# Two buffers of gathered sums in the pass over groups, and the gather issued ahead of the list writes

## What is computed

```
x1 = x + (sum over edges and self loops of alpha * xl[src]) @ W_up
s  = layernorm(x1) @ expert_tokens.T            # 8 scores, top 2
x2 = x1 + sum over the 2 experts of 0.5 * mlp_e(layernorm(x1))
```

## Time and profile before

| | us |
|---|---|
| median of three runs | 2071.64 |
| the profiled execution, its own time | 2070.93 |
| its span in the profile | 2069.0 |
| TensorE matmuls busy | 1657.0 (80%) |
| VectorE busy | 1310.2 (63%) |
| GpSimd busy | 783.9 (38%) |
| ScalarE busy | 774.3 (37%) |

### The profile page before, as it was taken

How to read it: one execution, slowest core, us unless ns; L and a number is a source line. 1 busy time by engine, 2 the same in 40 slices (tenths; PEclk the granted TensorE clock), 3 DMA queues, 4 the chain that set the end, 5 groups by cost and what they waited for, 6 DMA issues and landing times.

```text
span 2069.0 us, 27936 instructions
## 1 busy us (share of the span) xinstructions
PE 1657.0 (80%) x8625; PEld 1335.5 (65%) x8625; DVE 1310.2 (63%) x2446; ACT 774.3 (37%) x1342; POOL 783.9 (38%) x758
## 2 busy tenths in 40 slices
PE   4999999999586636887788783888888788788886
PEld 3788888888332325676567663667666676666665
DVE  4555555555266555666668773777777777776775
ACT  3444444443133520000100002555555555555554
POOL 1211222112488002554456542443444443443453
PEclk9999999999888776888788886999999999999999
DMA  9344444441544235899888854566665665566421
GB/s 242 85 135 124 119 119 119 119 133 47 158 119 113 74 126 129 223 227 217 200 219 216 206 157 119 157 193 177 180 175 166 170 177 171 168 171 179 115 52 34
DMA packets 128365, 311.76 MB, mean 151 GB/s; under 512 B 69455, under 2 KB 75981, under 8 KB 116651
## 3 DMA queue, kind: packets, MB, share of 16 engines
q1 hardware_dynamic: 58809, 181.56, 34.1%
q0 software_dynamic: 66208, 108.34, 19.0%
q10 hardware_dynamic: 3234, 20.48, 3.2%
HBM read 188.85 MB, written 138.85 MB: 158 GB/s over the span
## 4 chain that ended last, share of the span: by engine, by line
PE 47%; DMA 14%; DVE 13%; POOL 11%; issue 9%; ACT 5%; SPq 2%; DVEq 0%; POOLq 0%; ACTq 0%
PE psum L1531 12%; PE psum L1533 10%; PE psum L1532 10%; DMA agg<-node_table,from_idx 6%; DVE xt_lo L1448 4%; PE psum L1556 4%; DVE xb L1467 3%; DMA out<-xb,idx_in 3%; PE psum L1549 3%; POOL lists L651 2%; POOL agg L634 2%; PE psum L1812 2%; POOL xls L616 2%; DMA xb<-rows_x,idx_in 2%; POOL td L620 2%
## 5 line engine op out<-in xcount | busy, mean ns | idle before, releaser
L1531 PE MATMUL psum<-xt_hi,st_w 128*128 128x256 f32 x528 | 179.5, 340 | 142.5 <-DVE xt_lo L1448 138.7
L696 POOL DMA_INDIRECT out<-xb,idx_in x132 | 184.8, 1400 | 142.0 <-DVE xb L1467 109.5
L855 ACT ACTIVATE xt_hi<-psum 128x512 fp32r<-128x512 f32 x264 | 150.8, 596 | 228.8 <-PE psum L1812 215.7
L1448 DVE TENSOR_TENSOR xt_lo<-psum,xt_hi 128x512 fp32r<-128x512 f32 x264 | 175.6, 684 | 89.9 <-ACT xt_hi L855 77.6
L1531 PEld LDWEIGHTS psum<-xt_hi,st_w 128*128 128x128 f32 x528 | 103.7, 196 | 186.1 <-DVE xt_lo L1448 178.5
L827 ACT ACTIVATE aggt_hi<-psum 128x500 fp32r<-128x500 f32 x40 | 22.7, 587 | 450.0 <-PE psum L1728 450.0
L1288 DVE TENSOR_TENSOR cx<-cx,psum 125x512 f32<-125x512 f32 x160 | 108.8, 680 | 121.5 <-PE psum L1533 119.1
L959 DVE TENSOR_TENSOR axt_lo<-psum,axt_hi 128x500 fp32r<-128x500 f32 x160 | 108.5, 678 | 108.9 <-ACT axt_hi L728 95.0
L849 ACT ACTIVATE xn<-xb 128x1024 f32<-128x1024 f32 x132 | 156.3, 1232 | 54.8 <-DMA xb<-rows_x,idx_in 54.5
L1812 PE MATMUL psum<-ident,xn 128*128 128x128 f32 x1056 | 154.3, 281 | 23.1 <-ACT xn L849 23.1
L687 POOL DMA_INDIRECT xb<-rows_x,idx_in x132 | 140.1, 1062 | 85.6 <-POOL xb L683 54.0
(11 more groups left out here) (280 smaller groups left out, 4413.7 us busy)
## 6 DMA issues: line engine op xcount, KB each, us to landing
rows_x<-cx SPq DMA_DIRECT2D x20, 1806.0 KB
cx<-in_x SPq DMA_DIRECT2D x20, 1792.0 KB
ax<-in_x SPq DMA_DIRECT2D x19, 1792.0 KB
st_half<-experts SPq DMA_DIRECT2D x66, 512.0 KB
node_table<-trow ACTq DMA_DIRECT2D x19, 896.0 KB
node_table<-xld SPq DMA_DIRECT2D x10, 500.0 KB
st_half<-experts SPq DMA_DIRECT2D x66, 64.0 KB
rows_x<-cx SPq DMA_DIRECT2D x20, 209.6 KB
```

Of the source, the lines that this page charges most:

```text
L696: pool.indirect_dma_start(out=out[:, :], out_offset=bass.IndirectOffsetOnAxis(ap=idx_in[:, t % NI, s:s + 1], axis=0), in_=xb[:, b, s, 0:D] ...
L855: act.activation(xt_hi[:, 2 * q:2 * q + 2, :].rearrange("p k n -> p (k n)"), T_R[q % 2], ACT.Copy).then_inc(r_hi, 1)
L1448: dve.tensor_tensor(xt_lo[:, 2 * q:2 * q + 2, :].rearrange("p k n -> p (k n)"), T_R[q % 2], xt_hi[:, 2 * q:2 * q + 2, :].rearrange("p k n ...
L1531: pe.matmul(out_ap, left[0], right[0], start=start, stop=False, skip_group_check=True)
```

## The change

`agg` gets two buffers, chosen by g % 2, and a semaphore for each. A gather waits on `c_atp` for the transposes of the group two before instead of the one before. On GpSimd `gather_rows(g + 2)` stands ahead of `enlist(g - 1)`. `turns_p`, a semaphore that nothing waits on, is dropped, and its increments go to `turns`, on which nothing waits either.

```
-            ("agg", [P, J, HID], F32),
+            ("agg", [P, 2, J, HID], F32),
...
-        agg_loaded, list_put = sem("agg_loaded"), [sem("list_put0"), sem("list_put1")]
+        agg_loaded = [sem("agg_loaded0"), sem("agg_loaded1")]
+        list_put = [sem("list_put0"), sem("list_put1")]
...
-        turns, turns_p = sem("turns"), sem("turns_p")
+        turns = sem("turns")
...
             def gather_rows(g):
-                wait(pool, c_atp, KH * g)
+                wait(pool, c_atp, KH * (g - 1))
                 for j in range(J):
                     pool.indirect_dma_start(
-                        out=agg[:, j, :], out_offset=None, in_=t_half,
+                        out=agg[:, g % 2, j, :], out_offset=None, in_=t_half,
...
-                    ).then_inc(agg_loaded, 16)
+                    ).then_inc(agg_loaded[g % 2], 16)
...
             for g in range(NG):
                 if g >= 1:
                     rstd_c(g - 1)
-                    enlist(g - 1)
                 if g + 2 < NG:
                     gather_rows(g + 2)
+                if g >= 1:
+                    enlist(g - 1)
...
             def turn_agg(g):
-                pe.wait_ge(agg_loaded, 16 * J * (g + 1))
+                pe.wait_ge(agg_loaded[g % 2], 16 * J * (g // 2 + 1))
...
-                        last = pe.transpose(T_C[m][:, P * j:P * (j + 1)], agg[:, j, 128 * m:128 * (m + 1)],
+                        last = pe.transpose(T_C[m][:, P * j:P * (j + 1)], agg[:, g % 2, j, 128 * m:128 * (m + 1)],
```

More of the change, by code:

```diff
@@ L198, in build @@
             at3,
-            ("cx1", [P, J, ROW], F32), ("cx2", [P, J, ROW], F32), ("agg", [P, J, HID], F32),
+            ("cx1", [P, J, ROW], F32), ("cx2", [P, J, ROW], F32), ("agg", [P, 2, J, HID], F32),
             ("aggt_hi", [128, 2, KH, G], F32R), ("aggt_lo", [128, 2, KH, G], F32R))
@@ L583, in body @@
                 pool.wait_ge(map_put, 16 * (CPG * g + 1))
-                pool.sem_inc(turns_p, 1)
+                pool.sem_inc(turns, 1)
                 pool.tensor_copy(idx_now[:, 0:CPG], scat_idx[:, bass.ds(CPG * g, CPG)])
```

## The result

The changed kernel takes 2005.69 us (median of four runs, 2003.32 to 2012.03), beside 2072.32 us for the kernel before in the same runs. The ratio is 0.9681, 95% interval 0.9639 to 0.9723. The forecast was 2000 us.

A forecast was written before the change was run, and what follows sets the result against it. It took late gathered sums, issued behind list writes that wait for slot numbers, to bound pass C. From 2070.93 us, -6.2 for group 0 and -65.3 for 18 shorter periods gave 1999.4, say 2000 us; range 1977 to 2045.

The forecast's parts named there:

- What bounds the kernel before: Pass C: TensorE waits 76.4 us for gathered sums from group 1 on; the gather stands behind list writes awaiting slot numbers.
- Group 0: Start of pass C: the gather for group 1 goes out early, its 6.19 us wait goes; -6.2 us, bounds 0 and -7.6.
- The gather's place and landing: GpSimd issues it from 1.45 us after the score sum; sums land at 17.9 or 22.4, needed at 26.
- What is moved behind it: GpSimd's list writes lose nothing, the slot numbers coming at T + 7.6; VectorE's 11.1 us wait for the root goes.
- The new period: 18 periods of pass C fall from 22.53 to 18.9 us each, -65.3 us; bounds 17.56 and 22.53.
- (a): TensorE and VectorE limit in pass C: 18.5 us a period, the mean of five with little waiting, from 17.56 up.
- (b): DMA limit in pass C: share 0.83 over 422.54 us, read as 18.5 us of work for each of 19 groups.
- Its signs: Pass C: score sums some 340 us apart, `agg` waits under 10, slot wait under 3, DMA share near 0.97, 245 GB/s.
- Compute alone: Rival, pass C: DMA packs well and the period falls to 17.56 us, 1975 us in all; chance 0.15.
- The chain of store and load: Rival, SyncE: each load waits for a store to land, a hole of about 2.5 us, period 21.0, 2037 us; chance 0.23.
- No change: Rival, pass C: early gathers still wait for DMA engines behind loads of x, only group 0 gains, 2065 us; chance 0.06.
- Slower: Rival, pass C: gathers mixing with store and load lower the rate to 190 GB/s, 24.4 us a group, 2098 us; chance 0.06.

The follow-up runs named there:

- e2_order_only: Against the kernel before: gather ahead of the list writes, still one buffer of sums; 2015.34 us, ratio 0.9762.
- e1_buffers_only: Against the kernel before: two buffers of sums, gather still behind the list writes; 2058.5 us, ratio 0.9974.
- e6_late_gather_half_load: Two buffers, gather still behind the list writes, as in e1_buffers_only, with x loaded for two of four nodes from group 3 on; 2008.92 us, ratio 0.9713.
- e3_half_load: Changed kernel with x loaded for only two of four nodes of a partition from group 3 on; 1958.76 us, ratio 0.9503.
- e8_store_on_act: Changed kernel with the stores of a group's rows issued by ScalarE instead of SyncE; 1998.97 us, ratio 0.9652.
- e10_changed_again: The changed kernel run once more, unchanged, beside other kernels; 2002.79 us, ratio 0.9684.
- e4_split_halves: Changed kernel with each store and each load of x cut in halves, each half load behind its half store; 1995.39 us, ratio 0.9668.
- e7_more_bytes: Changed kernel with 0.92 MB of x copied from HBM to HBM beside each load of x, and waited for; 2044.00 us, ratio 0.9877.
- e5_by_node: Changed kernel with x loaded so that neighbouring partitions read neighbouring rows, same bytes and piece size; 2000.26 us, ratio 0.9670.
- e9_flat_load: Changed kernel with x from group 3 on loaded in one 16 KB piece for each partition instead of four of 4 KB; 2005.10 us, ratio 0.9681.
- e11_experts_late: Changed kernel with the weights of four of seven expert slots loaded behind the last load of x and split in the last two groups; 2013.61 us, ratio 0.9726.

## Why the prediction was right, and where it was off

*What bounds the kernel before.* Right. The sums were late because the gather was issued behind the list writes and their wait. e2_order_only shows it by the order alone, e1_buffers_only by the buffer alone. The loads of x in front of the late gather had a part in it (e6_late_gather_half_load).

*Group 0.* -6.2 us forecast, -7.4 measured (25.65 to 18.27), near the end of -7.6 that took in the slow matmuls behind the wait: the wait of 6.19 us is gone, and TensorE is busy 1.2 us less (19.46 to 18.27).

*The gather's place and landing.* Right. It was to be issued from T + 1.45 and is, from T + 1.7 (1047.39 for a score sum at 1045.71); the sums are there in time in all groups but one, which waits 2.9 us.

*What is moved behind it.* Right. The list writes start 3.12 us behind the gather, at the slot numbers; VectorE's wait for the root fell from 11.1 us to 0.8. e6_late_gather_half_load shows that this part can matter more than it seemed: with fewer bytes in the old order VectorE waits 37.2 us for the root, more than TensorE's 25.0 for the sums.

*The new period.* The term of the sum that was mis-sized: 18.9 us forecast, 19.34 measured (19.11 and 19.30 in two more profiles), 18 x 0.44 = 8 us too little, against which group 0 gave back 1.2. Both limits under it were off, and in opposite ways. (a) The compute limit was read as 18.5, and 17.56 as its lower bound, from the few periods of the old kernel without much waiting. With the DMAs relieved it is 16.93 (e3_half_load), and the first three periods of the changed kernel last 15.43 to 17.09. (b) The DMA limit was read as 18.5 from the share of 0.83. With a backlog it is 19.9 over 15 periods: the share of the kernel before counts busy engines, and it is no measure of bytes. The earlier trace rows already have it at 1.11, above a whole, at 146 GB/s (SyncE's next store is issued within that row, so it is not gathers and loads alone), and 240 to 243 GB/s go with shares of 0.88, 0.92 and 0.98 (e8_store_on_act, e10_changed_again at 241, e4_split_halves). The mean came out near because the early periods, three here and up to five in e10_changed_again, run at the compute limit, with x loaded ahead, and the rest at the DMA limit. That the nearness of 18.9 to 19.34 owes much to luck has to be said: one limit was 1.6 us too high, the other 1.4 too low, and they nearly cancelled.

*Its signs.* TensorE's wait for the sums (2.9 us, under 10) and VectorE's for the root (0.8) came as said. The score sums of groups 1 and 19 are 348.1 us apart, not some 340; the DMA share is 0.92, not 0.97, and the rate 239 GB/s, not 245. The wait for the slot numbers has a mean of 4.6 us (91.3 in 20 times) where under 3 was said: VectorE, which makes them, now waits for x itself.

*The figure for DMA.* By the rule that the prediction cited from the Trainium skill (DMA: Bandwidth & Descriptors, the anatomy of one DMA: about 2.0 us and 436 GB/s, a fit for a single DMA issued by GpSimd) the DMAs would let compute alone set the period. By e3_half_load that is 16.93 us, and the changed kernel takes 19.34; the pass runs at 236 to 243 GB/s in every version with both parts of the change and unchanged bytes. The trace disagrees with the rule for this mix, and the added copy of e7_more_bytes, at 320 to 370 GB/s, stays under it too.

*The rivals.* Compute alone: it holds for the first periods, then not. The chain of store and load: its sign was there, VectorE waiting 57.9 us for `cx` and loads issued 19 to 20 us apart behind a landed store, but the dry spell that was to cost 2.5 us costs nothing: filled (e4_split_halves), or with the stores in another queue (e8_store_on_act), the ratio does not move clear of the changed kernel's. No change: the early gather lands in time. Slower: the gathers beside the stores did not lower the rate, which rose to 239 GB/s.

*What stays open.* Why loads, stores and gathers together move some 240 GB/s. It is not the order of the rows in HBM (e5_by_node), the size of the piece (e9_flat_load), the gap between store and load, or one queue for both. A copy beside them, from HBM to HBM, adds its bytes at 320 to 370 GB/s, so the engines could move more than 240; whether the way into SBUF holds the rest back, no run tried by itself. Nor did a run try a fourth buffer of `cx`: in all of them a load of x waits for a store to land, also in e4_split_halves and e8_store_on_act. e11_experts_late, which moved 2.6 MB out of the stretch, gained less there than the bytes at 240 GB/s, so the expert loads may in part have run where nothing waited for them.

## What to carry to other kernels

Look at what stands in front of a late transfer on the engine that issues it: a gather whose buffer and indices are ready belongs ahead of any instruction that waits for this period's results, and the move can be worth far more than another buffer, here 53 of 65 us. After the move the next limit was the transfers; a DMA share under 1 in the old profile is not room that can be counted on, and the quickest test is to leave out part of the bytes. A deferred piece of work put in front of a needed one costs its whole wait, as the last group of the last kernel shows.

## What the runs showed of the hardware that was not expected

- The mean busy share of the DMA engines went from 0.92 to 0.98 with the halves, at 238 to 241 and 243 GB/s, and to 0.88 at 240 GB/s with the stores on ScalarE's queue. Busy engines were not a measure of bytes.
- Reading x in 4 KB or 16 KB pieces, or from neighbouring instead of distant rows, made no difference that the runs can tell (0.9681 and 0.9670 beside 0.9681, 0.9684 and 0.9672).
- 0.92 MB copied inside HBM beside each load of x cost 2.5 to 2.8 us in the periods that the DMAs set, 320 to 370 GB/s, while 87 MB of loads, stores and gathers took 365 us, 239 GB/s.
- TensorE kept a mean clock of 0.91 over 320 us in which it was busy for 99% of the time (e3_half_load): also without gaps it does not hold 1.0 in this pass. Of the 19 batches of 24 small score matmuls (8 columns each) that follow group 0's, 15 are followed by a stretch at 0.50 (1.2 GHz), of about 3 us in 13 of them and over 6 in two; behind the other four the clock stays at 1.0. The periods go with it: 16.3 to 17.1 us with a short low stretch, 18.4 and 18.5 with a long one, 15.5 to 16.4 without. In the kernel before, show the lower level in the same place.
